# An image-tower kernel on one core: a piece of a tile is requested only after the same piece of the preceding tile has landed

## The reference

```python
pooled = x.reshape(B, C, n, K, n, K).sum(axis=(3, 5))      # B=64, C=12, n=14, K=16
h = einsum('bcij,ce->bije', pooled, channel_weights).reshape(B, 196, 192)
h = h + attention(layernorm(h), W_qkv, b_qkv)
h = h + feed_forward(layernorm(h), w_fc * C0, b_fc * c0b, w_proj * C1, b_proj * c1b)
```

## Time and profile before

| | |
|---|---|
| time of three executions | 493.6, 494.9, 494.9 us (median 494.9) |
| the profiled execution | 494.9 us, of which the span of instructions is 492.8 us |
| busy: PE, DVE, ACT, POOL | 425.7, 381.7, 287.8, 255.0 us |
| transfers of `xs` | 336 of 448 KB, issued from 6.0 to 407.1 us |
| median time from the issue of a transfer of `xs` to its landing | 12.4 us |
| data moved | 166.65 MB |

### The profile page before, as it was taken

The page is one execution under the profiler, slowest core; times in us unless marked ns, Lnnn a source line. Parts: engine busy times, 40 slices in busy tenths (PEclk is TensorE's granted clock), DMA queues, the critical chain, the costliest instruction groups (busy, mean ns, idle before and its releaser), DMA issues.

```text
span 492.8 us, 10971 instructions
## 1 busy us (share of the span) xinstructions
PE 425.7 (86%) x4558; PEld 362.9 (74%) x4558; DVE 381.7 (77%) x288; ACT 287.8 (58%) x494; POOL 255.0 (52%) x194
## 2 busy tenths in 40 slices
PE   5976453996899999899898989798999899999996
PEld 4544232784678888788787978687888779888896
DVE  1788898899799998899989898989898999420000
ACT  1022044534878676758583858575868466877821
POOL 1032313703659293818374758475656657485940
PEclk9999555696699999989998999999999989999999
DMA  8999999999999999999999999999999997101101
GB/s 241 335 404 401 404 402 402 403 402 406 402 401 401 403 403 403 403 399 404 397 403 398 404 395 400 396 401 402 397 403 399 400 391 310 34 26 33 43 26 50
DMA packets 56661, 166.65 MB, mean 338 GB/s; under 512 B 5972, under 2 KB 13030, under 8 KB 56612
## 3 DMA queue, kind: packets, MB, share of 16 engines
q1 hardware_dynamic: 56612, 165.95, 87.7%
HBM read 156.29 MB, written 9.63 MB: 337 GB/s over the span
## 4 chain that ended last, share of the span: by engine, by line
DMA 47%; DVE 20%; PE 17%; SPq 7%; issue 4%; POOL 3%; ACT 1%; DVEq 0%; ACTq 0%
DMA xs<-x 47%; DVE pooled L480 18%; PE ps L609 17%; SPq L412 5%; POOL h_lo L1123 2%; DVE phat_tok L498 1%; POOL inv L1100 0%; POOL inv L1114 0%; ACT probs L967 0%; ACT out_sb L1024 0%; PE ps L786 0%; SPq L429 0%; DVE prod L489 0%; ACT h_hi L1018 0%; DVEq L475 0%
## 5 line engine op out<-in xcount | busy, mean ns | idle before, releaser
L480 DVE TENSOR_REDUCE pooled<-xs 128x28 f32<-128x1792 f32 x144 | 328.8, 2323 | 29.3 <-DMA xs<-x 29.3
L1123 POOL TENSOR_TENSOR h_lo<-h_f,h_hi 128x784 fp32r<-128x784 f32 x96 | 176.9, 1868 | 86.6 <-ACT h_hi L1018 86.6
L609 PE MATMUL ps<-w_hi,h_hi 128*98 128x192 f32 x768 | 207.9, 271 | 1.3 <-POOL h_lo L1123 1.1
L609 PE MATMUL ps<-w_lo,h_hi 128*98 128x192 f32 x768 | 196.9, 256 | 0.0
L609 PE MATMUL ps<-w_hi,h_lo 128*98 128x192 f32 x768 | 196.7, 256 | 0.0
L609 PEld LDWEIGHTS ps<-w_hi,h_hi 128*98 128x98 f32 x768 | 128.9, 168 | 16.7 <-issue 14.2
L609 PEld LDWEIGHTS ps<-w_lo,h_hi 128*98 128x98 f32 x768 | 129.4, 168 | 0.0
L609 PEld LDWEIGHTS ps<-w_hi,h_lo 128*98 128x98 f32 x768 | 129.1, 168 | 0.0
L1009 ACT ACTIVATE h_f<-ps 128x784 f32<-128x784 f32 x96 | 74.8, 824 | 21.7 <-PE ps L609 21.6
L1018 ACT CAST h_hi<-h_f 128x784 fp32r<-128x784 f32 x96 | 79.5, 851 | 0.1
L1100 POOL TENSOR_TENSOR inv<-var,minus_half 98x8 f32<-98x8 f32 x16 | 26.2, 1636 | 70.4 <-DVE var L494 70.3
(11 more groups left out here) (119 smaller groups left out, 355.4 us busy)
## 6 DMA issues: line engine op xcount, KB each, us to landing
xs<-x SPq DMA_DIRECT2D x336, 448.0 KB, 12.4
out<-out_sb SPq DMA_DIRECT2D x32, 294.0 KB
rows_sb<-wfc SPq DMA_DIRECT2D x1, 576.0 KB, 5.5
out_sb<-wproj SPq DMA_DIRECT2D x1, 576.0 KB, 10.4
h_f<-wqkv SPq DMA_DIRECT2D x1, 432.0 KB
cf<-const_full SPq DMA_DIRECT2D x1, 264.0 KB, 3.0
h_f<-const_paired SPq DMA_DIRECT2D x1, 153.0 KB, 3.3
cr<-const_rows SPq DMA_DIRECT2D x1, 83.2 KB
```

The costliest lines, as they stand in the source:

```text
L480: dve.tensor_reduce(pooled[:, n % 2, t, GRID * first:GRID * end].rearrange("p (i j) -> p i j", j=GRID), runs, AX.XY, ALU.add).then_inc(red ...
L609: return pe.matmul(o, a, b, start=start, stop=stop, skip_group_check=shared)
L1123: pool.tensor_tensor(h_lo[:, m % 2, t], h_f32[:, t], h_hi[:, m % 2, t].bitcast(F32), ALU.subtract).then_inc(h_lo_ready, 1)
```

## The change

Before SP issues a piece of a tile from the third on, it now also waits until each run of the same piece of the preceding tile (which lies in the other slot) has landed. The wait on `reduced` stays; the order of SP's stream, the sizes, the buffers and all other engines' instructions stay.

```diff
@@ -418,6 +418,9 @@ load_chunk
                 if tile >= RING:
 
                     sp.wait_ge(reduced, PER_TILE * (tile - RING) + chunk + 1)
+
+                    for i in range(*CHUNKS[chunk]):
+                        sp.wait_ge(x_landed[(tile - 1) % RING][i], 16 * ((tile - 1) // RING) + 16)
                 for i in range(*CHUNKS[chunk]):
                     load(n, t, i)
```

## The result

The changed kernel takes 496.55 us (median of 10 executions, 494.3 to 497.7), the kernel before 493.55 us in the same measurement (10 executions, 492.5 to 495.7). The ratio is 1.0052, 95% interval [1.0036, 1.0069]: slower by 2.6 us. Measured again later, beside other kernels, it was 1.0028 [1.0002, 1.0053]. Where the executions of a kernel fell into a faster and a slower group, as those of e10_three did, ratios are of the faster group. The prediction was no change.

The account below looks back on a forecast made before the run. It took full DMA engines (about 400 GB/s, DVE close behind) to bound the load stage, then a tail of PE, ACT and POOL work. All terms were 0: 494.9 us + 0 = 494.9 us, range 493.0 to 498.0.

Parts of the forecast that it names:

- The naive reading of the chain: Load stage: 12 us of transfer latency lie in a loop, so whoever asks later lands later; the prediction called it queueing.
- Landings stay where they are: DVE, PE and tail: `xs` lands when it did, so order, waits and tail keep their times; cost 0.
- a full queue reaches it at the same moment: Output sends in SP's stream: issued up to 5.9 us later, yet landing no later because queue order is unchanged; cost 0.
- This had stood among the rivals: Lost cushion between DMA engines: with seven runs, one to three hold-ups no longer overlap, 1.1 to 3.3 us; chance 0.12.
- one such packet fits into the margin: Argument against the lost cushion: a queue q8 packet, 1.1 us on one DMA engine, fits into the third piece's margin.
- The dry queue: Rival at the third piece: release to landing exceeds 5.7 us; half a us too much costs 23 us; chance 0.07.
- I take the first: Third piece: chose the lower bound, 3.0 us from issue to landing, margin 2.7 us, so no gap and cost 0.
- The upper bound of 5.1 us: Third piece: quickest landing of any run, among the first seven behind the weights' transfers; leaves 0.6 us of margin.
- The sends: Output sends in SP's stream: issued up to 5.9 us later but landing no later, so ACT does not stall; cost 0.
- SP's waits: Line 412: seven more waits a tile cost 0; waiting passes from DVE to DMA and roughly doubles from 128.5 us.
- Issue instructions: SP's issues of transfers: the longest falls from 2840 ns to below 1 us; no gain, since nothing waits for them.
- Less crowding, faster: Rival in the load stage: fewer runs under way give 403 GB/s throughout, 2 us gained, 492.8 us; faster had chance 0.10.

Follow-up runs that it names:

- e10_three: Changed kernel, but a third piece waits for the first run of its own tile, leaving three runs ahead; ratio 1.0734 to the kernel before, +36 us.
- e3_third: Kernel before with the new wait on third pieces (runs 4 to 6) only; 495.95 us, ratio 1.0031.
- the two pairs meant to prove it: Kernel before and changed kernel, each with 25 extra GpSimd loads: 506.3 and 509.53 us; each with 25 extra one-row copies: 547.46 and 548.95 us.
- e5: Kernel before without the sends of the first twelve groups; 476.92 us, ratio 0.9655.
- e6: Changed kernel without the sends of the first twelve groups; 478.47 us, ratio 0.9707.
- changed again: The changed kernel, unaltered, measured once more beside later kernels; 494.22 us, ratio 1.0028 to the kernel before.
- e2_five: Changed kernel with the wait on the piece two back in the order, at most five runs under way; 582.78 us, ratio 1.1794 to the kernel before.
- e4_met: Kernel before with as many added waits, on runs of the tile about to be overwritten, already landed; 493.46 us, ratio 0.999.

## Why the prediction was wrong

**The naive reading of the chain.** Refuted as predicted: requests moved 5.6 us later from 216 to 300 us (13.0 to 7.4; 5.9 forecast), and 46 tiles did not cost 46 times that, but 2.6 us in all.

**The step that failed** is "Landings stay where they are, so DVE's order, the 29.3 us of waits and the tail do too". It followed from treating the 16 DMA engines as one queue: "a full queue reaches it at the same moment". The landings did not stay: with the third-piece wait the load stage grew, and the sum had put that at 0. What it measures is 1.7 us by the load stages of the traces (390.5 in three traces with the third-piece wait, 388.8 to 389.3 in four without a loss), 1.4 to 2.6 us by the two measured ratios. The theory that is left for it: the slowest engine is not always the same one; an engine that is ahead and finds nothing requested loses its lead, and what later holds it up is then paid by all. This had stood among the rivals, with a price of 1.1 to 3.3 us, and got 0.12; only because of it does the stated range hold the measured 496.55 us; the forecast itself was 494.9 and no change. The point against it, "one such packet fits into the margin", used a margin of 2.7 us. The spread that is left is 2.4 us, and two hold-ups of 1.1 us on one engine, before it has regained its lead, would nearly fill it; no record shows such a pair.

How firmly this stands: that the engines run 2.4 instead of 7.9 us apart, that the load stage is 1.7 us longer with it, that the wait of the third piece is enough for it, and that SP's instructions, the bare limit of seven and the uneven sends are not the reason, is shown, the last two by load stages that are 1.2 and 2.0 us apart in single traces. A dry queue in front of run 4 is made unlikely by the gaps without a send (1.142 and 1.145 us for 1.137). A rare gap elsewhere in the piece, as e10_three has it before run 6, is not excluded for the changed kernel (1.17 us in both its traces, 1.15 before, standard errors 0.02); in e3_third, which loses as much, that gap is 1.12. That the loss consists of hold-ups that no longer overlap is argued. It fits the doubled loss with added ones; the two pairs meant to prove it did not, since the records name no engine and the added copies all cost as if on one engine. The equal load stages without sends (e5 and e6) speak against it and are not explained. So the cause stays open.

The first ratio, at least 1.8 us by its interval, may hold more than these 1.7 us. From the last landing of `xs` to the end, which the change doesn't touch, the traces have 73.3 us (before), 72.4 (changed), 71.3 (changed again) and 71.2 to 71.8 in the four others of the table. So single executions differ by up to 2 us in the tail, and the load stages are the steadier measure.

**The dry queue.** Right, as far as the gaps above show it, that it would not set in, and wrong by how much. "I take the first" put the need from issue to landing at 3.0 us, 4.0 for a busy memory, and the margin at 2.7. With an all but empty queue under full traffic a run took 4.4 us in the median (e2_five), which leaves 1.3 us. The upper bound of 5.1 us was the nearer one. The Trainium skill's figure for a busy memory (DMA: Bandwidth & Descriptors, Latency and other measured facts) would have made it 4.8 us, an estimate from that page; the measured median is 0.4 us below it, and decides. The need of the first run isn't the whole of it, though: three runs ahead cover 4.6 us, more than 4.4, and e10_three lost 36 us all the same, mostly at the last run of the piece.

**The sends.** As predicted. They go out later, and in the changed kernel's trace ACT waits for no transfer; the waits of SP at its send line (now 429) are still nearly all tail, 74.1 us for 80.4.

**SP's waits.** Cost 0, confirmed by e4_met. They grew from 128.5 to 185.4 us (170.2 + 15.2), not to the double. **Issue instructions:** the longest is 1.3 us, not below 1. **Time to landing:** 7.3 us median, within 6.5 to 7.5. **Less crowding, faster:** refuted; at 10.4, 8.7 and 7.4 us to landing no kernel got faster.

## What to carry to other kernels

A transfer here was complete with the last of 16 increments, and requests made ahead did two things: they covered the latency of the next one, and they let the engines run apart (7.9 us with the deep queue, 2.4 with the shallow one). That the second is worth time, because a hold-up of one engine then isn't paid by all, is the likeliest reading and not proven. Six runs ahead of each request lost nothing measurable, four lost 0.3 to 0.5%, three 7%. When a bound on what is under way must be set, ask what is left at the moment of the next request, and ask in small pieces: seven under way, requested one by one, cost nothing measurable where seven requested in twos and threes did.

## What was not expected of the hardware

Against the kernel before, three runs ahead (448 KB each) cost 36 us and four 1.4 to 2.6 us: the edge is within one run. And it was mostly the last run of the late piece that paid (a gap of 1.66 us for 1.15), not the first. A load of 17 rows from GpSimd's queue was spread over several DMA engines, while single rows of 61,396 B cost as if all had fallen on one and the same (25 in a row, 2.3 us each, +54 us; the records name no engine). A send of 98 partitions costs more than one of 96 and one of 2: 2.2 us in 32 sends.
